# Recurrence of a four-layer stack: the next chunk but one has its normed tokens turned in steps 13 and 14 of a chunk, in place of 14 and 15

## The reference

```
xa = layer_norm(x)                                   # "normed tokens"
sx = [state, xa[:-1]] - xa                           # token shift
xxx = tanh((xa + sx * maa_x) @ maa_w1)               # -> five mixtures
xm_f = xa + sx * (maa_stack_f + xxx_f @ maa_w2_f)    # f = k, w, v, r, g
w = exp(-exp(time_decay + tanh(xw @ td_w1) @ td_w2))
r, k, v = xr @ Wr.T, xk @ Wk.T, xv @ Wv.T ; g = silu(xg @ Wg.T)
for t in tokens:                                     # per head, 8 x 8 state
    out_t = r_t @ (u * k_t v_t^T + s)
    s = k_t v_t^T + w_t * s
x = x + (group_norm(out) * g) @ Wo.T
x = x + sigmoid(xr2 @ Wfr.T) * (relu(xk2 @ Wfk.T)**2 @ Wfv.T)   # on layer_norm(x)
```

## Time and profile before

| | us |
|---|---|
| median of 3 runs (1978.57 to 1981.2) | 1978.76 |
| the profiled execution | 1977.81 |
| its span | 1975.7 |
| TensorE busy / weight loads busy | 1875.9 / 1551.0 |
| VectorE / ScalarE / GpSimd busy | 1113.9 / 1044.2 / 996.6 |
| mean granted clock of TensorE | 0.974 |

### The profile page before, as it was taken

How to read it: one execution, slowest core, us unless ns; L and a number is a source line. 1 busy time by engine, 2 the same in 40 slices (tenths; PEclk the granted TensorE clock), 3 DMA queues, 4 the chain that set the end, 5 groups by cost and what they waited for, 6 DMA issues and landing times.

```text
span 1975.7 us, 39304 instructions
## 1 busy us (share of the span) xinstructions
PE 1875.9 (95%) x15088; PEld 1551.0 (79%) x15088; DVE 1113.9 (56%) x2104; ACT 1044.2 (53%) x1945; POOL 996.6 (50%) x1140
## 2 busy tenths in 40 slices
PE   7999999988897899999999999999999998999999
PEld 5777779534454788899999999999999987977788
DVE  4566656389989654444454444454444455755654
ACT  3565543434343656665665656556566554345532
POOL 6777731366654543654544544545454434347630
PEclk9999999889998999999999999999999999999999
DMA  6000010000000222232232232232232210000000
GB/s 236 2 2 2 2 57 1 1 0 1 1 1 11 91 81 75 83 104 83 82 106 82 81 107 82 81 107 82 81 102 87 81 60 22 22 29 16 2 11 33
DMA packets 61847, 108.11 MB, mean 55 GB/s; under 512 B 7008, under 2 KB 42336, under 8 KB 60256
## 3 DMA queue, kind: packets, MB, share of 16 engines
q1 hardware_dynamic: 60784, 103.38, 16.7%
q10 hardware_dynamic: 880, 2.22, 0.3%
HBM read 103.47 MB, written 2.10 MB: 53 GB/s over the span
## 4 chain that ended last, share of the span: by engine, by line
PE 84%; DVE 7%; issue 4%; POOL 3%; ACT 2%; DMA 0%; DVEq 0%; SPq 0%; ACTq 0%; POOLq 0%
PE banks L862 18%; PE banks L891 9%; PE banks L934 9%; PE banks L627 7%; PE banks L644 7%; PE banks L466 7%; PE banks L923 6%; PE banks L904 4%; PE banks L475 3%; PE banks L548 2%; PE banks L523 2%; PE banks L505 2%; PE banks L534 2%; PE banks L912 1%; PE banks L460 1%
## 5 line engine op out<-in xcount | busy, mean ns | idle before, releaser
L1983 POOL TENSOR_TENSOR w_lo<-w2ring,w_hi 128x512 fp32r<-128x512 f32 x128 | 176.1, 1376 | 254.9 <-ACT w_hi L1128 254.9
L2067 POOL TENSOR_TENSOR wo_lo<-wo_ring,wo_hi 128x256 fp32r<-128x256 f32 x128 | 94.6, 739 | 254.6 <-ACT wo_hi L1337 254.6
L1808 DVE TENSOR_REDUCE nmax<-banks 128x4 f32<-128x260 f32 x128 | 54.3, 424 | 280.2 <-PE banks L904 280.2
L1794 DVE TENSOR_TENSOR v<-banks,dbv 128x512 f32<-128x512 f32 x128 | 88.5, 692 | 201.6 <-PE banks L891 200.7
L1337 ACT ACTIVATE wo_hi<-wo_ring 128x256 fp32r<-128x256 f32 x128 | 53.3, 417 | 197.6 <-PE banks L934 197.5
L934 PE MATMUL banks<-wo_hi,c_hi 128*128 128x256 f32 x512 | 145.5, 284 | 4.4 <-DVE c_lo L1801 4.4
L934 PE MATMUL banks<-wo_lo,c_hi 128*128 128x256 f32 x512 | 145.4, 284 | 0.0
L934 PE MATMUL banks<-wo_hi,c_lo 128*128 128x256 f32 x512 | 145.3, 284 | 0.0
L1324 ACT ACTIVATE k<-banks,cols 128x512 f32<-128x512 f32 x128 | 88.1, 688 | 79.4 <-PE banks L862 79.4
L923 PE MATMUL banks<-PT,v 128*128 128x128 f32 x1024 | 125.3, 276 | 3.4 <-issue 3.4
L923 PEld LDWEIGHTS banks<-PT,v 128*128 128x128 f32 x1024 | 120.3, 192 | 3.8 <-issue 3.8
(11 more groups left out here) (235 smaller groups left out, 5525.1 us busy)
## 6 DMA issues: line engine op xcount, KB each, us to landing
w2ring<-in_w SPq DMA_DIRECT2D x128, 384.0 KB, 4.1
b2ring<-in_b SPq DMA_DIRECT2D x128, 128.0 KB, 4.5
wo_ring<-in_wo SPq DMA_DIRECT2D x128, 128.0 KB, 4.3
mlp_w<-in_mlp SPq DMA_DIRECT2D x6, 1024.0 KB, 7.1
wl<-in_wres SPq DMA_DIRECT2D x1, 2688.0 KB, 9.0
X<-in_x_in SPq DMA_DIRECT2D x4, 512.0 KB, 11.1
wb<-in_wres SPq DMA_DIRECT2D x2, 1024.0 KB, 10.8
ctxT<-in_ctx_in SPq DMA_DIRECT2D x4, 512.0 KB, 19.8
```

The source lines that it names most:

```text
L1794: V.tensor_tensor(v2[:, :, 2 * half:2 * half + 2, :].rearrange("p s i d -> p i s d"), held(("v2", p, half))[:, :].rearrange("p (i s d) -> ...
L1983: G.tensor_tensor(w2_lo[:, n % 2, :], w2ring[:, n % HR, 0:2 * KT * P], w2_hi[:, n % 2, :].bitcast(f32), ALU.subtract).then_inc(S["l2_wlo"], 1)
L2067: G.tensor_tensor(wo_lo[:, n % 2, :], wo_ring[:, n % WR, :], wo_hi[:, n % 2, :].bitcast(f32), ALU.subtract).then_inc(S["l2_wolo"], 1)
```

## The change

In the lists of TensorE and ScalarE, and in both places of each (the preparing steps and chunks 0 to 2), the two halves of `front` are issued in steps 13 and 14 in place of 14 and 15. What is issued, its waits and signals, and its place at the end of its step stay the same.

```diff
@@ TensorE, preparing steps (chunks 0 to 2: the same with L1_FIRST + c + 2)
                         before(0, j)
-                        if j >= 14:
-                            front(L1_FIRST + 1, j - 14, MIDDLE)
+                        if j in (13, 14):
+                            front(L1_FIRST + 1, j - 13, MIDDLE)
                         yield 1
@@ ScalarE, chunks 0 to 2 (preparing steps: the same with L1_FIRST + 1)
                             if j == 12:
                                 normed(L1_FIRST + c + 2)
-                            if j >= 14:
-                                front(L1_FIRST + c + 2, j - 14)
+                            if j in (13, 14):
+                                front(L1_FIRST + c + 2, j - 13)
```

More of the change, by code:

```diff
@@ L835, in rwkv @@
                         if c + 1 < CHUNKS:
-                            if j >= 14:
-                                front(L1_FIRST + c + 2, j - 14, MIDDLE)
+                            if j in (13, 14):
+                                front(L1_FIRST + c + 2, j - 13, MIDDLE)
                         else:
@@ L1245, in rwkv @@
                             normed(L1_FIRST + 1)
-                        if j >= 14:
-                            front(L1_FIRST + 1, j - 14)
+                        if j in (13, 14):
+                            front(L1_FIRST + 1, j - 13)
                         yield 1
```

## The result

The changed kernel takes 1968.61 us (median of 5 runs, 1967.2 to 1970.87) against 1978.76 us for the kernel before (5 runs, 1977.19 to 1981.2): ratio 0.9947, 95% interval 0.9933 to 0.9962, so 10.2 us less. A second set of runs gave 0.9950 (0.9938 to 0.9963).

What follows compares the result with a forecast made beforehand. VectorE was taken to bound the recurrence. Gains of 2.0 + 1.45 - 0.15 at the three chunk borders and 0 before the first chunk sum to 3.3 us, 1978.76 to 1975.5 us; range 1971.0 to 1979.5.

Steps and rivals of the forecast that it cites:

- The bound: In the recurrence VectorE is the bound, with a product and a scan per step for 64 steps.
- the removed wait: VectorE's two waits for hT at the token shift, 4.7 us together, up to 2.4 us each, should be gone.
- what is next: With the shift stall gone, the gate's second eviction and the first-state copy behind it set VectorE's next product.
- Displacements: Moved transposes delay VectorE's products: step 15 of chunk 0 by 0.4 us, step 0 of chunk 2 by 0.55.
- Border 3: Chunk 2 into 3: no VectorE wait for hT there; next product at 572.9 in place of 572.73, 0.15 us lost.
- The size of the terms at borders 1 and 2: Gains at chunk 0 into 1 and chunk 1 into 2: 2.0 and 1.45 us.
- The clock: TensorE's half-clock dips, six in the recurrence, near 3 us each with neighbours; not in the sum.
- (a): Rival: a half-clock dip falls away because two VectorE stalls are gone; 6.3 us gained, 1972.5; chance 0.20.
- (b): Rival: one half-clock dip more; 0.3 us gained, 1978.5; chance 0.08.
- dips placed otherwise: Sign of being wrong: TensorE's half-clock dips in the recurrence fall at other places in the profile after.
- (c): Rival: the stall is only handed on to the gate's eviction; 0 to 1.5 us lost, about 1979; chance 0.06.
- (d): Rival: output projection and gate fall to half clock at chunk borders 2 and 3; 5.5 us slower, 1984.3; chance 0.06.

Runs made afterwards that it cites:

- border 3 alone: Kernel before, with only chunk 2 having the two halves of front in steps 13 and 14: 1977.31 against 1977.66 us, ratio 0.9996.
- the changed kernel delayed: Changed kernel with 80 in place of 48 warm-up transposes at the start: 1972.7 us, ratio to before 0.9976.
- border 2 alone: Kernel before, with only chunk 1 having the two halves of front in steps 13 and 14: 1973.2 against 1978.35 us, ratio 0.9970.
- the GpSimd wait on before: Kernel before, GpSimd's product of step 1 of chunks 0 to 2 waiting for VectorE's first mixture: 1974.4 against 1978.35 us, ratio 0.9981.
- border 1 alone: Kernel before, with only chunk 0 having the two halves of front in steps 13 and 14: 1974.35 against 1978.35 us, ratio 0.9977.
- after with GpSimd waits: Changed kernel, GpSimd's step 1 products (chunks 0-2) and last-chunk steps 1 and 9 held behind VectorE's mixtures: 1968.95 us, ratio to before 0.9952.

## Why the prediction was wrong, step by step

**The bound, the removed wait, what is next:** right. Both waits for hT are gone and no other has taken their place for their whole length; banks cost nothing (F0 shows no wait for VectorE); the gate's second eviction is next at border 1, and at border 2 it ends together with the shift.

**Displacements:** at border 1 the product of step 15 was to be 0.4 us late, measured 0.14. At border 2 0.55 us, measured 0.45 (0.14 at product 31 and 0.30 at 32). Both were high. Border 3, forecast at -0.15 (a loss), gave 0.32: 0.34 later by product 48, 0.66 earlier at 49. The displacement was 0.2 less than I put in, and the product follows the end of the gate's eviction after 0.11 us and not after 0.4. Before the first chunk: forecast zero, measured 0.2 to 0.4 gained in three traces of the changed kernel, against up to 0.3 between traces of before.

**The size of the terms at borders 1 and 2, the first failed step.** Forecast were 2.0 and 1.45; measured are 3.18 and 2.73. Up to the first product after the shift the sum was near: 2.18 up to product 17 (2.32 less 0.14 of displacement), and 1.71 up to 33 (2.15 less 0.44). The rest is 1.01 at each, one step further on, where the prediction took the distances to stay ("after each border every TensorE and ScalarE operation waits for a scan or a mixing product of VectorE"). Its bound for a border, VectorE's idle time of 2.38 us, was passed for the same reason: what went was busy time. In before, GpSimd's product of step 1 ran beside VectorE's mixture L1617 and held it up by 1.0 us. In the kernel after, the mixture comes first and GpSimd's product is late enough, for another reason: its ring of five slots is full until TensorE's total (L682), which now stands later relative to VectorE (at border 1 it starts 1.76 us behind product 17, in before 0.05):

```profile
508.18 1.39 DVE L1617 SCALAR_TENSOR_TENSOR xm<-sxT,cols,hT 128x512 f32<-128x512 f32 x2
509.20 1.50 POOL L2024 TENSOR_TENSOR rsZ<-stS,r1T 128x512 f32<-128x512 f32 x1 [3.03 <-PE banks L682]
```

The wait put on GpSimd in the kernel before shows the price alone: 1.03 at each border.

The same meeting stood just ahead of it, in a stretch that the prediction took as fixed. It took 1.63 us for the pair of shifts at both borders. In before at border 1 the second of the pair, of 8 columns, ran beside GpSimd's shift and took 1.00 us:

```profile
452.18 1.52 POOL L1972 TENSOR_TENSOR sxT<-hT 128x504 f32<-128x504 f32 x1 [2.93 <-ACT hT L1015]
...
452.74 1.00 DVE L1605 TENSOR_TENSOR sxT<-ctxT,hT 128x8 f32<-128x8 f32 x1
```

In the kernel after it takes 0.18 there, the pair 1.22, and it would have let the product go 0.56 us before the gate's copy did. At border 2 it meets another product of GpSimd and takes 1.25, the pair 1.82.

**The clock, the second and larger failed step.** It was put at nothing in the sum and left to rivals (a) and (b), as one dip less or more. Measured were two stretches gone, together 3.36 us, in both traces of the changed kernel. Without them the gain would have been about 6.5 us, which the range holds. The prediction's own sign of being wrong, dips placed otherwise, came true. The matmuls against the earlier trace rows: L682 is still at half clock (1.94 us; it takes 1.06 at full clock in other steps), but the eight projection matmuls behind it run at full clock, 3.70 in place of 5.83 us.

```profile
532.02 1.94 PE L682 MATMUL banks<-rsZ,consts 128*32 128x512 f32 x8 [0.15 <-POOL rsZ L2024]
...
533.88 3.70 PE L466 MATMUL banks<-xm,wl 128*128 128x512 f32 x8
```

For "bonus", TensorE's rows of border 3 alone show it: the feed-forward matmuls run from 575.56, and the bonus matmuls take 0.6 us per group, where in before the first four groups took 0.94 to 1.20. First before, then border 3 alone:

```profile
581.05 0.50 PE L671 MATMUL banks<-v_hi,sel_r 128*128 128x512 f32 x1 [0.50 <-DVE stS L1657]
...
583.57 1.20 PE L696 MATMUL banks<-consts,rku 128*128 128x128 f32 x4 [1.79 <-DVE rku L1643]
...
585.41 1.06 PE L696 MATMUL banks<-consts,rku 128*128 128x128 f32 x4
```

```profile
575.56 3.70 PE L466 MATMUL banks<-xm,wl 128*128 128x512 f32 x8 [1.67 <-DVE xm L1712]
...
581.26 0.68 PE L696 MATMUL banks<-consts,rku 128*128 128x128 f32 x4 [1.55 <-DVE rku L1643]
582.23 0.61 PE L696 MATMUL banks<-consts,rku 128*128 128x128 f32 x4
```

"Bonus" ran at full clock in all nine traces in which border 3 was edited (in one of them, of the changed kernel delayed, the feed-forward matmuls ahead of it were at half clock), and at half clock in eight of nine in which it wasn't. In the edited ones the feed-forward matmuls start 1.0 us later relative to VectorE (5.13 in place of 4.12 us after product 49), and the pause of 0.50 us between them and the next vb matmuls is gone. That this pause alone decides is ruled out by the two traces of border 2 alone. Both have it, and the bonus matmuls run at half clock in the first and at full clock in the second (first trace, then second):

```profile
574.45 0.50 PE L671 MATMUL banks<-v_hi,sel_r 128*128 128x512 f32 x1 [0.50 <-DVE stS L1657]
...
577.93 1.02 PE L696 MATMUL banks<-consts,rku 128*128 128x128 f32 x4
```

```profile
574.73 0.50 PE L671 MATMUL banks<-v_hi,sel_r 128*128 128x512 f32 x1 [0.50 <-DVE stS L1657]
...
578.22 0.61 PE L696 MATMUL banks<-consts,rku 128*128 128x128 f32 x4
```

"k" is not tied to an edited border: border 3 alone lacks it with nothing edited up to there, the GpSimd wait on before lacks it with all of `front` in place, border 1 alone has it, and after with GpSimd waits has it. So of the 9.9 us, 6.2 are the border edits', shown one by one; 1.6 go with border 3 in 17 of 18 traces; 1.7 belong to the program as a whole, and the last 0.3 lie behind. What places the stretches stays open.

The whole sum is then 3.3 forecast, 0.9 from the terms that were cut too small (0.2, 0.3 and 0.5 at the three borders), 2.0 from GpSimd's products, 3.4 from the clock and 0.3 behind.

Rival (a) named the clock, but with 6.3 us in place of 9.9, and its reason is not borne out: border 1 alone removes a stall and no stretch, and border 3 alone, where VectorE waited for no hT, lacks both. That it had the right sign is luck. (b), (c) and (d) didn't happen: the recurrence has five half-clock stretches in place of six, the stall was not handed on whole, and no border ran at half clock. The Trainium skill ("TensorE: Matmul & The Clock Gate", "HAM oscillation — how this bites in real kernels") says that idle gaps of TensorE bring the half rate back. No run here shows which gaps did it: a pause went with a stretch at border 3, but the same pause stands in both traces of border 2 alone, and the stretch in one.

## What to carry to other kernels

Follow a removed stall until the two schedules run in parallel again, not to the next instruction of the waiting engine: two engines that met at one operation may no longer meet. Look for operations of which the same shape takes 0.74 us in one place and 1.76 in another; here each was a mixture beside a GpSimd product, worth 1.0 us. The short shift L1605, 0.17 us in one place and 1.00 or 1.25 in another, was the same sign, within the 1.63 us that the forecast took as fixed. And where TensorE alternates between its two clocks, a small change can move half-clock stretches by an amount as large as itself. Most of this repeats from one execution of a program to the next, but not all (one stretch of 1.61 us came and went in border 2 alone), so take two traces before crediting an edit with it, and judge edits of a microsecond by distances between instructions.

## What the runs showed of the hardware

A VectorE operation with two SBUF inputs (L1617, two 128x512 operands) takes 0.74 us alone and 1.76 when a GpSimd product (1.27 us alone) runs into it; GpSimd's then takes 1.69. The Trainium skill ("SBUF — State Buffer", "SBUF: two separate sides") states that the pair of ports that both use is locked for a whole instruction against a GpSimd operation that reads SBUF; the trace agrees: the excess of 1.02 us is most of a GpSimd product, and the mixture ends 0.55 us behind the GpSimd product that it met. In before none of the 40 mixtures that read a bank instead (L1632, 0.72 to 0.75 us) was held up. The short shift L1605, with two SBUF inputs of 128x8, takes 0.17 us alone and 1.00 to 1.25 beside GpSimd.

In the recurrence TensorE's half-clock stretches mostly repeat in a program: in the five traces of before, on several chips and with everything up to 4.5 us apart, "k" and "bonus" stand within 0.03 us of the first trace. They need not: border 2 alone had "bonus" at half clock in one trace and at full clock in the other (1.61 us), with all products up to there within 0.04 us. And they differ between two programs even ahead of the first instruction in which these differ: border 3 alone lost 2.57 us in products 18 to 26 in both of its traces, where before has no such loss in any of five. What fixes them was not found.
